# The third feed-forward written out with its output matmuls two groups behind, and shorter chains to the choice of experts

## The reference

```python
x = _layernorm(x + _L0_attn_ref(...))   # attention, 16 heads of 16
x = _layernorm(x + _L0_ffn_ref(...))    # experts
x = _layernorm(x + _L1_attn_ref(...))   # attention, 16 heads of 128
x = _layernorm(x + _L1_ffn_ref(...))    # second feed-forward: 128 experts as mixtures of 8 bases, top 4
x = _layernorm(x + _L2_attn_ref(...))   # convolution and a running sum
x = _layernorm(x + _L2_ffn_ref(...))    # third feed-forward
x = _layernorm(x + _L3_attn_ref(...))   # differential attention
x = _layernorm(x + _L3_ffn_ref(...))    # fourth feed-forward: 32 experts, top 4
```

```python
h = silu(x @ w_gate) * (x @ w_up)       # 2048 x 1024
h_sparse = _sparsify_2to4(h)            # of each 4 neighbours the 2 largest by magnitude, ties to the lower index
out = h_sparse @ w_down                 # 2048 x 256
```

```python
probs = softmax(xt @ w_router)                       # second: 128 experts
topk_p, topk_idx = top_k(probs, 4)
topk_w = topk_p / (sum(topk_p) + 1e-8)               # fourth: without the 1e-8
```

## Time and profile before

| | |
|---|---|
| median of 3 runs | 2937.93 us (2935.14 to 2938.83) |
| profiled execution | 2937.16 us, of it span 2935.4 |
| busy over the span | PE 84%, PEld 65%, DVE 67%, ACT 47%, POOL 16% |
| second feed-forward, first hidden matmul to last down | 1396.8 to 1566 us |
| third feed-forward, first matmul to last copy | 1686.0 to 1901.5 us |
| fourth feed-forward, first hidden matmul | 2470.7 us |

### The profile page before, as it was taken

How to read it: one execution, slowest core, us unless ns; L and a number is a source line. 1 busy time by engine, 2 the same in 40 slices (tenths; PEclk the granted TensorE clock), 3 DMA queues, 4 the chain that set the end, 5 groups by cost and what they waited for, 6 DMA issues and landing times. The chain is left out here.

```text
span 2935.4 us, 42983 instructions
## 1 busy us (share of the span) xinstructions
PE 2473.6 (84%) x14000; PEld 1912.8 (65%) x14000; DVE 1958.4 (67%) x4408; ACT 1389.4 (47%) x3760; POOL 483.6 (16%) x406
## 2 busy tenths in 40 slices
PE   7998999879999999995998687777777756999997
PEld 5665666558777777774676565555554435877876
DVE  3665588866566565665456757657778775777777
ACT  4664577654545445453222232167777663333322
POOL 2442100020000000000221000046666560000000
PEclk9998999989999999997999888888888876999999
DMA  4001000010110001102000000000000003000000
GB/s 157 7 11 58 1 0 0 0 44 22 32 32 29 14 21 32 32 29 100 1 0 0 0 0 0 25 28 5 4 7 4 4 1 140 1 0 0 0 0 29
DMA packets 28084, 63.79 MB, mean 22 GB/s; under 512 B 4208, under 2 KB 16496, under 8 KB 26480
## 3 DMA queue, kind: packets, MB, share of 16 engines
q1 hardware_dynamic: 28016, 62.93, 6.1%
HBM read 54.27 MB, written 2.10 MB: 19 GB/s over the span
## 5 line engine op out<-in xcount | busy, mean ns | idle before, releaser
L2059 ACT ACTIVATE l3a_pr<-psum,l3a_nm 128x128 f32<-128x128 f32 (+1 forms) x512 | 207.0, 430 | 109.3 <-DVE l3a_nm L2167 109.3
L113 DVE TENSOR_TENSOR x_sb<-psum,x_sb 128x512 f32 (+2 forms) x48 | 41.6, 866 | 203.4 <-PE psum L1044 104.9
L2436 ACT ACTIVATE l3f_sg<-psum 128x512 f32<-128x512 f32 x96 | 57.3, 597 | 238.8 <-PE psum L2392 238.8
L1105 ACT ACTIVATE l1a_pr<-psum,l1a_nb,l1a_rq 128x128 f32<-128x128 f32 (+1 forms) x256 | 127.2, 509 | 80.0 <-DVE l1a_nb L1191 74.5
L2389 PE MATMUL psum<-l3f_x_hi,l3f_w_hi 128*128 x384 | 153.8, 400 | 7.4 <-DVE l3f_w_lo L2472 7.4
L2167 DVE TENSOR_REDUCE l3a_nm<-psum 128x2 f32<-128x256 f32 (+1 forms) x256 | 124.7, 550 | 50.5 <-PE psum L1891 50.1
L2390 PE MATMUL psum<-xT,l3f_w_hi 128*128 x384 | 152.3, 397 | 0.0
L2391 PE MATMUL psum<-l3f_x_hi,l3f_w_lo 128*128 x384 | 151.6, 395 | 0.0
L1365 POOL TENSOR_TENSOR l1f_acc<-l1f_t 128x512 f32<-128x512 f32 x4 | 6.3, 1572 | 848.3 <-DVE l1f_t L1428 848.3
L2012 POOL TENSOR_TENSOR l3a_pr<-l3a_pr,w_l3a_mask 128x1024 f32<-128x1024 f32 x32 | 78.0, 2438 | 368.5 <-ACT l3a_pr L2059 368.5
L2403 PE MATMUL psum<-l3f_w_hi,l3f_h_hi 128*128 128x256 f32 x384 | 127.3, 332 | 7.9 <-DVE l3f_h_lo L2490 7.9
(11 more groups left out here) (459 smaller groups left out, 7495.8 us busy)
## 6 DMA issues: line engine op xcount, KB each, us to landing
l1a_kT<-l1a_o_dram SPq DMA_DIRECT2D x64, 256.0 KB, 2.7
w_l3f_all<-l3f_all_dram SPq DMA_DIRECT2D x1, 9216.0 KB, 25.7
w_l0f_w<-l0f_w_dram SPq DMA_DIRECT2D x2, 2048.0 KB, 10.0
w_l1f_all<-l1f_all_dram SPq DMA_DIRECT2D x1, 2560.0 KB, 9.4
cf_sb<-xT SPq DMA_DIRECT2D x9, 256.0 KB, 2.5
x_sb<-x_dram SPq DMA_DIRECT2D x1, 2048.0 KB, 8.5
l0a_xc<-xT SPq DMA_DIRECT2D x8, 256.0 KB, 2.5
w_l1a_q<-l1a_q_dram SPq DMA_DIRECT2D x1, 2048.0 KB, 8.0
```

Source lines behind the costliest of these rows:

```text
L1105: last = nc.scalar.activation(pr[:, n % 2, i, s], S[n % 2][:, i, s], ACT.Exp, bias=nb[:, n % 2, t, i:i + 1], scale=rq[:, t, 2 * n + i:2 * ...
L2059: last = nc.scalar.activation(pr[:, r, a, g, k], S[:, g, k], ACT.Exp, bias=nm[:, i % 2, g, t:t + 1], accum_out=sums[:, r, a, g, t:t + 1])
```

## The change

*Third feed-forward.* The loop over four chunks is gone on all three engines: the eight sets (g = 0 to 7, two a chunk) are written out. `hh` has three homes in place of two, the output two pairs of banks (4 and 5, 6 and 7), `x_lo` a tile of its own. TensorE runs the four hidden blocks of set g, then the down matmuls of set g - 2. VectorE's pruning is cut into `compare`, `beaten_by_both`, `choose` and `keep`, placed between the products of later sets. `ab_free` tells ScalarE that the magnitudes were read, `used` counts sets that the down matmuls have read.

*Routing.* The exponentials are no longer scaled before the choice; the sum of the four chosen is taken over `top`, which holds them, and in the second feed-forward the small constant is multiplied by the sum of all. The subtractions for `x_lo` move behind the chain, in chunks, and TensorE waits for a chunk in each turn of its loop. In the second the copy of `coT` is shared by VectorE and ScalarE, and the first two weight splits move before it.

```diff
@@ l1_ffn, tensor
-                pe.wait_ge(coT_ready, 1)
+                pe.wait_ge(coT_ready, 2)
                 w["late"](pe)
-                pe.wait_ge(xlo_ready, NCH)
                 with pe.Fori(0, NCH) as b:
+                    pe.wait_ge(xlo_ready, b + 1)
@@ l1_ffn, scalar
                 weights_hi(1)
+                act.wait_ge(coT_ps, 1)
+                nc.scalar.activation(coT[:, 2 * CN:4 * CN].rearrange("p (a n) -> p a n", a=2), psum[:, 6:8, :], ACT.Copy).then_inc(coT_ready, 1)
@@ l1_ffn, vector
-                for j in range(NCH):
+                def tokens_lo(j):
                     cols = slice(j * CN, (j + 1) * CN)
...
                 dve.wait_ge(ex_ready, 1)
-                st.do(nc.vector.reciprocal(wsum[:, :], sums[:, :]))
-                st.do(nc.vector.tensor_tensor(pb[:, :, 0:E], pb[:, :, 0:E], bc(wsum[:, :], 2, E), ALU.mult))
...
-                st.do(nc.vector.tensor_reduce(wsum[:, :], co[:, :, :], AX.X, ALU.add))
-                st.do(nc.vector.tensor_scalar(wsum[:, :], wsum[:, :], EPS, None, ALU.add))
+                st.do(nc.vector.tensor_reduce(wsum[:, :], top[:, :, 0:TOP], AX.X, ALU.add))
+                st.do(nc.vector.scalar_tensor_tensor(wsum[:, :], sums[:, :], EPS, wsum[:, :], ALU.mult, ALU.add))
...
-                dve.wait_ge(coT_ps, 1)
-                nc.vector.tensor_copy(coT[:, :].rearrange("p (a n) -> p a n", a=4), psum[:, 4:8, :]).then_inc(coT_ready, 1)
...
                 weights_lo(0, 0)
                 weights_lo(1, 1)
+                tokens_lo(0)
+                dve.wait_ge(coT_ps, 1)
+                nc.vector.tensor_copy(coT[:, 0:2 * CN].rearrange("p (a n) -> p a n", a=2), psum[:, 4:6, :]).then_inc(coT_ready, 1)
+                for j in range(1, NCH):
+                    tokens_lo(j)
@@ l2_ffn, tensor
-                with pe.Fori(0, NCH) as b:
...
+                def down(g):
+                    b, s = g // SETS, g % SETS
+                    if s == 0:
+                        if b >= 2:
+                            pe.wait_ge(z_ready, b - 1)
+                        for a in range(2):
+                            mm(Y[b % 2][:, 2 * a:2 * a + 2, :], c["zero"], bc(c["idb"], 1, 4), start=True, stop=False)
+                    pe.wait_ge(kept, g + 1)
...
+                for g in range(NS + 2):
+                    if g < NS:
+                        for i in range(4):
+                            hidden(4 * g + i)
+                    if g >= 2:
+                        down(g - 2)
@@ l2_ffn, scalar
+                for n in range(4 * NS):
...
+                    nc.scalar.activation(sg[:, n % 2, :], bank(n % 2), ACT.Silu).then_inc(sg_ready, 1)
+                    weights_hi((n + 2) % NH)
+                    if n >= 4 and n % 4 == 0:
+                        magnitudes(n // 4 - 1)
+                magnitudes(NS - 1)
@@ l2_ffn, vector
+                def product(n):
+                    e, g = n % NH, n // 4
+                    dve.wait_ge(sg_ready, n + 1)
+                    if n % 4 == 0 and g >= HOMES:
+                        dve.wait_ge(used, g - HOMES + 1)
+                    nc.vector.tensor_tensor(hh[:, g % HOMES, n % 4 // 2, n % 2, :], sg[:, n % 2, :], bank(2 + n % 2), ALU.mult).then_inc(hh_ready, 1)
+                    weights_lo((e + 2) % NH, n + 2)
...
+                for g in range(NS + 1):
+                    if g < NS:
+                        product(4 * g)
+                    if g >= 2:
+                        keep(g - 2)
+                    if g < NS:
+                        product(4 * g + 1)
+                    if g >= 1:
+                        compare(g - 1)
+                    if g < NS:
+                        product(4 * g + 2)
+                    if g >= 1:
+                        beaten_by_both()
+                    if g < NS:
+                        product(4 * g + 3)
+                    if g >= 1:
+                        choose()
+                    if g >= 4 and g % 2 == 0 and g < NS:
+                        output(g // 2 - 2)
+                keep(NS - 1)
+                output(NCH - 2)
+                output(NCH - 1)
@@ l3_ffn, tensor
-                pe.wait_ge(xlo_ready, X0 + 1)
                 with pe.Fori(0, NCH) as b:
+                    pe.wait_ge(xlo_ready, b + X0 + 1)
@@ l3_ffn, scalar
-                    last = nc.scalar.activation(pb[:, t, 0:E], LOGITS[:, t, :], ACT.Exp, bias=nm[:, t:t + 1], accum_out=sums[:, t:t + 1])
+                    last = nc.scalar.activation(pb[:, t, 0:E], LOGITS[:, t, :], ACT.Exp, bias=nm[:, t:t + 1])
@@ l3_ffn, vector
-                dve.wait_ge(xhi_ready, X0 + 1)
-                nc.vector.tensor_tensor(x_lo, xT[:, :, :], x_hi[:, :, :].bitcast(F32), ALU.subtract).then_inc(xlo_ready, 1)
...
-                st.do(nc.vector.reciprocal(wsum[:, :], sums[:, :]))
-                st.do(nc.vector.tensor_tensor(pb[:, :, 0:E], pb[:, :, 0:E], bc(wsum[:, :], 2, E), ALU.mult))
...
-                st.do(nc.vector.tensor_reduce(wsum[:, :], cw[:, :, :], AX.X, ALU.add))
+                st.do(nc.vector.tensor_reduce(wsum[:, :], top[:, :, 0:TOP], AX.X, ALU.add))
...
+                dve.wait_ge(xhi_ready, X0 + 1)
+                tokens_lo(0)
                 dve.wait_ge(c3T_ps, 1)
...
                 weights_lo(0, 0)
+                for j in range(1, NCH):
+                    tokens_lo(j)
```

More of the change, by code:

```diff
@@ L1391, in _, with weights_lo @@
                     nc.vector.tensor_tensor(x_lo[:, :, cols], xT[:, :, cols], x_hi[:, :, cols].bitcast(F32), ALU.subtract).then_inc(xlo_ready, 1)
+                def weights_lo(e, count):
+                    dve.wait_ge(whi_ready, count + 1)
+                    nc.vector.tensor_tensor(w_lo[:, e % 2, :, :], w["all"][:, e, :].rearrange("p (k n) -> p k n", n=P),
+                                            w_hi[:, e % 2, :, :].bitcast(F32), ALU.subtract).then_inc(wlo_ready, 1)
                 dve.wait_ge(ex_ready, 1)
[L1393 to L1394 removed]
                 for t in range(NT):
@@ L1587, in l2_ffn @@
         bank = lambda i: psum[:, i, :]
-        Y = psum[:, 6:8, :].rearrange("p a (t n) -> p (a t) n", t=2)
+        Y = [psum[:, a:a + 2, :].rearrange("p a (t n) -> p (a t) n", t=2) for a in (4, 6)]
         h_ps = sem("h_ps")
@@ L1605, in _, with hidden @@
                 mm = nc.tensor.matmul
-                def clear_output():
-                    for a in (6, 7):
-                        mm(bank(a), c["zero"], bc(c["idb"], 1, 4), start=True, stop=False)
+                def hidden(n):
+                    b, e = n // NH, n % NH
+                    if e == 0:
+                        pe.wait_ge(xlo_ready, b + 1 + X0)
+                    if n >= 2:
+                        pe.wait_ge(hh_ready, n - 1)
+                    pe.wait_ge(wlo_ready, n + 1 + W0)
+                    chunk = slice(b * CN, (b + 1) * CN)
+                    for first, bk in ((0, 0), (KD, 2)):
+                        for k in range(KD):
+                            hi, lo = w_hi[:, e % 2, first + k, :], w_lo[:, e % 2, first + k, :]
+                            mm(bank(bk + e % 2), hi, x_hi[:, k, chunk], start=(k == 0), stop=False)
+                            mm(bank(bk + e % 2), hi, x_lo[:, k, chunk], start=False, stop=False)
+                            last = mm(bank(bk + e % 2), lo, x_hi[:, k, chunk], start=False, stop=(k == KD - 1))
+                    last.then_inc(h_ps, 1)
@@ new lines, in down @@
+                def down(g):
[6 more added lines that the diff above has]
+                    pe.wait_ge(kept, g + 1)
+                    for t in range(CH):
+                        for i in range(4):
+                            last = mm(Y[b % 2][:, t, :], hh[:, g % HOMES, i // 2, i % 2, t * P:(t + 1) * P], w["down"][:, 4 * s + i, :],
+                                      start=False, stop=(s == SETS - 1 and i == 3 and t % 2 == 1))
+                    last.then_inc(used, 1)
@@ L1650, in _ @@
                 weights_hi(1)
[L1651 to L1665 removed]
+                for n in range(4 * NS):
+                    act.wait_ge(h_ps, n + 1)
+                    if n >= 2:
+                        act.wait_ge(hh_ready, n - 1)
+                    nc.scalar.activation(sg[:, n % 2, :], bank(n % 2), ACT.Silu).then_inc(sg_ready, 1)
[3 more added lines that the diff above has]
+                magnitudes(NS - 1)
             @block.vector
             def _(dve):
[L1669 to L1670 removed]
+                st = Steps(dve, steps, 0)
+                st.begin(0)
                 for j in range(NCH):
```

120 lines of the change are left out of this document (41 added, 79 removed).

## The result

The changed kernel takes 2869.57 us (median of four runs, 2865.92 to 2871.77) against 2936.59 us for the kernel before in the same comparison: a ratio of 0.9765, 95% interval 0.9754 to 0.9777. It is faster, and 0.4 us from the forecast of 2870. The profiled execution took 2871.77 us, with a span of 2870.0 us.

The account below looks back on a forecast made before the run. In the third feed-forward TensorE and VectorE took turns; overlapped, TensorE would bound it, by little. Gains of 55.2 there, 9.3 and 2.9 in the second and fourth routings, 67.4 in all, took 2937.2 to 2870 us, range 2859 to 2887.

Parts of the forecast that it names:

- What bounds the stage: Third feed-forward: no engine is full; TensorE and VectorE take turns where they could overlap, with 47.9 us of TensorE waits.
- rival 1: Third feed-forward: the engines don't mesh, each of eight groups loses another 1.5 us; 2882 to 2885 us, chance 0.15.
- the term for groups 3 to 7: Third feed-forward, steady groups: TensorE loses 0.9 us in all, where a hidden block comes late.
- The set of down matmuls, 6.86: Third feed-forward: one set of down matmuls at 2.4 GHz takes 6.86 us, counted eight times, 54.9 us.
- Waits in groups 1 and 2, 4.1: Third feed-forward: VectorE already prunes, no down matmuls cover it yet; TensorE loses 4.1 us.
- Tail, 10.2: Third feed-forward's end: idles of 3.2 and 3.5 us before the last two down sets, output 3.5; together 10.2 us.
- The clock in the last set: Third feed-forward, last down set: nothing taken for a low clock after the idle, 3.2 us as upper bound.
- The same sum from the other side: Third feed-forward's gain: waits fall from 47.9 to 11.7 us, which is 36.2; the rest, 19, is the low clock's cost.
- Second routing, 9.3: Second feed-forward's routing: earlier maxima 5.5, shorter sum 2.1, halved copy and moved split 1.75; 9.3 us gained, bounds 7.4 and 10.5.
- Fourth routing, 2.9: Fourth feed-forward's routing: scaling gone 1.05, closer exponentials 1.3, shorter sum 0.5; 2.9 us gained, bounds 1 and 4.
- 2: Third feed-forward: the loop's three turns held waits for code, 9.3 us more gained; 2861 us, chance 0.03.
- 3: Third feed-forward: written-out code comes too slowly, 74.4 us lost at 24 hidden blocks; 2944 us, chance 0.04.

Follow-up runs that it names:

- kept-busy version: The changed kernel with 14 zero-weight matmuls into a free bank before the wait of the last set of down matmuls: 2868.99 us, ratio 0.9772.
- lag-one version: The changed kernel with down matmuls one group behind the hidden blocks instead of two: 2947.82 us, ratio 1.0038.
- routing-only run: The changed kernel with the third feed-forward of the kernel before, both routings as changed: 2925.08 us, ratio 0.9952.

## Why the prediction was right, and where it was off

*What bounds the stage.* Right: with the same code in both, the order alone is worth 234.6 against 181.8 us; with the downs only one group behind, all of the gain went and 27 us more with it (242.3 against 215.5 before).

*The sum of the stage, step by step.* Set 0 is the first set of down matmuls. The forecast column is added up from the prediction's terms, and its rows are rounded:

| us | forecast | measured |
|---|---|---|
| first matmul to set 0 | 38.6 | 38.7 |
| set 0 to set 5 | 90.5 | 91.7 |
| set 5 to set 6 | 10.5 | 10.0 |
| set 6 to set 7 | 10.4 | 10.7 |
| set 7 to the end | 10.4 | 13.2 |

*Set 0 to set 5.* No idle is named there, but the four hidden blocks of a group take 11.41 to 11.49 us in place of 10.88. The prediction's own sign for rival 1, hidden blocks more than 2.8 us apart on average in groups 3 to 7, is thus met, at 2.86. The products do come just behind the block that needs them, but at a cost of some 0.5 us a group and not 1.5, and part of it is paid back by the down sets, which take 6.72 from their start to the next hidden block. Net it is 2.1 us where the term for groups 3 to 7 had 0.9.

*The set of down matmuls, 6.86.* The size is near, by luck. The row it was read from the earlier trace rows was cut off by its window; the whole set is this:

```profile
1836.09 8.65 PE L1635 MATMUL psum<-w_l2f_down,l2f_hh 128*128 128x256 f32 x32 [5.34 <-DVE l2f_hh L1703]
```

It is not a set at 2.4 GHz with three records missing: its first three are before the window, and its grant is 0.82. No set of the kernel before ran at full clock throughout (8.65 to 10.09 us, 73.5 for the eight; after, 59.4).

*Waits in groups 1 and 2, 4.1.* Right: 3.07 of named idle, 4.0 from start to start.

*Tail, 10.2.* From the end of set 5 (1813.29) to set 6 it is 3.05 us, forecast 3.2, but the clearing of the output lies inside that time (2.46 are left as idle), and the sum had it beside it: 0.5 too much. Before set 7 it is 3.52, as forecast.

*The clock in the last set.* This is the mis-sized term. The forecast took nothing, with 3.2 as the bound, because 3.5 lay nearer to 2.55, read as harmless, than to 5.59. It cost 2.6 to 2.8 in three profiles (9.79, 9.82 and 9.96 against 7.17), and the kept-busy version shows that it is the clock and not the last `keep`. The 2.55 was not harmless either: the row ends with four matmuls, and the clock fell behind them, as windows of the kernel before show (columns as in the earlier trace rows):

```profile
1599.00:1600.00 1.00, 0.80 (x4) 0.72 (x5) 0.96 (x4) 0.00 (x0) 0.00 (x0) 1.00 0.00 0
1600.00:1601.00 1.00, 1.00 (x7) 0.97 (x5) 0.81 (x6) 0.00 (x0) 0.00 (x0) 0.59 0.00 0
1601.00:1602.00 1.00, 1.00 (x4) 0.81 (x4) 0.15 (x1) 0.00 (x0) 0.00 (x0) 0.50 0.00 0
```

With the 1.2 of the steady groups it makes most of the miss of the stage, 164.3 instead of 160.3.

*The same sum from the other side.* It does not hold term by term. It had 36.2 us from shorter waits and 19 from the clock. The named waits of TensorE inside the stage went from 47.9 to 9.1, which is 38.8, and its busy time fell by 12.7 with as many records. The 19 was what the total left over and not a reading.

*Second routing, 9.3.* The three terms are right: 5.5, 2.1 and, for the halves, 1.1. The size of the whole depends on the clock under the router. With the router at 7.38 us, as before, the chain took 28.0 in the kept-busy and 28.4 in the lag-one version, 9.3 and 8.9 less, where the text of the routing-only run asked for 9.0 or more: that is about the forecast, and the rival that a step was over-priced (7.5 whatever the router takes) falls; with 8.78 to 9.01, in the nine other profiles with the new routing, it took 29.7 to 30.0. The stage gains 8.4 on average over eleven profiles of the new routing (214.5) and two of the old (222.9).

*Fourth routing, 2.9.* Right within 0.1 on its chain: the reads that went brought the exponentials to 0.18 us apart, as estimated, and the second weight split (2409.55) comes in time, with no idle of TensorE behind the first block. The stage gained another 1.3 behind the first hidden matmul: 0.9 of it is TensorE's busy time (436.3 to 435.4, with 2408 records in both), 0.3 its waits for weight splits (7.4 to 7.1). Why the busy time fell stays open.

*Rivals.* 1 fell by its size, though its mechanism is there in small (above), and the last down did run cold. The profile after was to show waits for `keep` in groups 0, 6 and 7; there are none in group 0. 2 and 3 fell by the straight version in the old order. The Trainium skill, "Runtime: NRT & Kernel Launch", section "Instruction fetch mechanics", has a taken branch stall where its target lies outside what has been fetched, and prefers full unrolling for that reason. Here three turns fewer saved nothing that can be seen: 2924.41 us straight, 2925.08 looped, the stage 234.6 and 233.0. This does not show that a branch is never dear, only that it was not in this loop.

*Not tested.* How much of the gain needs the pruning cut into pieces, and how much the third home of `hh` and the second pair of banks: every version with the lag of two has them all.

## What to carry to other kernels

When two engines take turns, count each one's work per group before changing either. If both sums are below the period that you want, a lag can give each engine the other's work of an earlier group: here that took away 38.8 of 47.9 us of waits, and 12.7 us of TensorE's busy time with them, since the clock rose. One group of lag too few cost more than the turns did, since the last product's whole pruning then lay open. Look at the fill and the tail by themselves: the last set is where an idle was left, where the clock fell, and where halving the last choose, keep and down still brought 5 us. And read a row beyond the edge of its window before resting a price on it: two prices of this prediction, the full-speed set and the harmless idle, came from rows that ended too soon.
